# Attention plus mixture of experts on one core: batch 1's scores without stacks, a new order for the first six periods, dummies on TensorE, and a joined router operand

## What is computed

```python
def _L0_xattn_ref(Q, K, V, W_Q, W_K, W_V, W_O):      # 8 heads of 16
    q = proj_split(Q, W_Q); k = proj_split(K, W_K); v = proj_split(V, W_V)
    scores = jnp.einsum('bhqd,bhkd->bhqk', q, k) / jnp.sqrt(jnp.float32(dh))
    attn = jax.nn.softmax(scores, axis=1)             # over the heads
    ctx = jnp.einsum('bhqk,bhkd->bhqd', attn, v)
    ctx = ctx.transpose(0, 2, 1, 3).reshape(b, s, d)
    return jnp.einsum('bsd,ed->bse', ctx, W_O)
...
x = x + _L0_xattn_ref(_layernorm(x), ctx_1024, ctx_1024, W_Q, W_K, W_V, W_O)
# experts: E = 8, the best 2 of each token, hidden width 256
logits = jnp.einsum('btd,de->bte', x, Wr) + br
topv, topi = jax.lax.top_k(logits, K)
gates = jax.nn.softmax(jnp.where(sel_mask, logits, neg_inf), axis=-1)
h = jax.nn.relu(jnp.einsum('btd,edh->bteh', x, W1) + b1)
out = jnp.einsum('bte,bteh,ehd->btd', gates, h, W2) + jnp.einsum('bte,ed->btd', gates, b2)
x = x + out                                           # its input is _layernorm(x)
```

## Time and profile before

| | us |
|---|---|
| median of 3 runs | 211.32 (210.55 to 213.79) |
| the profiled execution, its own time | 210.83 |
| span of the profiled execution, first to last instruction | 209.0 |
| VectorE busy in it | 166.0 |
| ScalarE busy in it | 132.3 |
| GpSimd busy in it | 110.0 |

### The profile page before, as it was taken

The page is one execution under the profiler, slowest core; times in us unless marked ns, Lnnn a source line. Parts: engine busy times, 40 slices in busy tenths (PEclk is TensorE's granted clock), DMA queues, the critical chain, the costliest instruction groups (busy, mean ns, idle before and its releaser), DMA issues.

```text
span 209.0 us, 4976 instructions
## 1 busy us (share of the span) xinstructions
PE 199.0 (95%) x1752; PEld 176.3 (84%) x1752; DVE 166.0 (79%) x445; ACT 132.3 (63%) x316; POOL 110.0 (53%) x132
## 2 busy tenths in 40 slices
PE   6999888698999999999999999999999999999994
PEld 6846775686899889997999799988998999789993
DVE  5398779889789999988888988798989978365542
ACT  2236847796578858687668767575767685345541
POOL 8603657869795475439661966285738672010000
PEclk9999999999999999999999999999999999999999
DMA  6549695725434233424241306050000000000000
GB/s 195 137 137 291 178 266 161 206 86 159 109 102 100 78 100 105 102 75 104 98 106 53 124 14 183 13 175 4 0 3 25 0 2 28 0 3 2 28 0 25
DMA packets 20248, 18.70 MB, mean 89 GB/s; under 512 B 1760, under 2 KB 18688, under 8 KB 20224
## 3 DMA queue, kind: packets, MB, share of 16 engines
q1 hardware_dynamic: 17472, 16.91, 28.2%
q10 hardware_dynamic: 2752, 1.48, 2.7%
HBM read 11.83 MB, written 6.55 MB: 88 GB/s over the span
## 4 chain that ended last, share of the span: by engine, by line
PE 91%; DVE 3%; ACT 2%; issue 1%; POOL 1%; DVEq 0%; POOLq 0%; ACTq 0%
PE y_ps L416 28%; PE h_ps L403 21%; PE score_ps L343 7%; PE misc_ps L362 6%; PE score_ps L331 6%; PE h_ps L351 4%; PE score_ps L265 3%; PE misc_ps L300 2%; PE misc_ps L383 2%; PE score_ps L320 2%; PE score_ps L403 2%; PE misc_ps L371 1%; PE misc_ps L270 1%; PE misc_ps L309 1%; PE misc_ps L289 1%
## 5 line engine op out<-in xcount | busy, mean ns | idle before, releaser
L670 ACT ACTIVATE hT<-h_ps,b_sb 128x256 f32<-128x256 f32 x118 | 49.4, 470 | 34.5 <-PE h_ps L403 33.4
L416 PE MATMUL y_ps<-w_sb,hT 128*128 128x128 f32 x512 | 68.4, 276 | 0.0
L416 PEld LDWEIGHTS y_ps<-w_sb,hT 128*128 128x128 f32 x512 | 63.3, 191 | 3.4 <-issue 2.0
L1152 POOL TENSOR_TENSOR half_sum<-e_sb 128x512 f32<-128x512 f32 x28 | 36.9, 1320 | 34.0 <-ACT e_sb L642 33.6
L911 DVE TENSOR_TENSOR attn<-e_sb,e_rcp 128x1024 f32<-128x1024 f32 x32 | 42.8, 1341 | 3.5 <-ACT e_rcp L653 3.3
L903 DVE TENSOR_REDUCE shift_m<-score_ps 128x128 fp32r<-128x1024 f32 x32 | 38.7, 1213 | 2.4 <-PE score_ps L331 1.2
L403 PE MATMUL h_ps<-x1T_hi,w_lo 128*128 128x256 f32 x118 | 37.7, 320 | 1.3 <-ACT hT L670 0.6
L642 ACT ACTIVATE e_sb<-score_ps 128x1024 f32<-128x1024 f32 x32 | 32.8, 1024 | 5.4 <-PE score_ps L343 5.2
L974 DVE SCALAR_TENSOR_TENSOR acc<-y_ps,gates,acc 128x128 f32<-128x128 f32 x96 | 29.0, 343 | 8.3 <-PE y_ps L416 6.9
L403 PE MATMUL h_ps<-x1T_lo,w_hi 128*128 128x256 f32 x118 | 33.1, 280 | 0.0
L403 PE MATMUL h_ps<-x1T_hi,w_hi 128*128 128x256 f32 x118 | 33.0, 279 | 0.0
(11 more groups left out here) (113 smaller groups left out, 286.8 us busy)
## 6 DMA issues: line engine op xcount, KB each, us to landing
k_scratch<-k_parts SPq DMA_DIRECT2D x14, 256.0 KB, 2.6
k_stack<-k_scratch SPq DMA_DIRECT2D x14, 256.0 KB, 4.0
q_stack<-q_scratch SPq DMA_DIRECT2D x28, 128.0 KB, 2.7
q_scratch<-q_parts SPq DMA_DIRECT2D x7, 256.0 KB, 2.5
w_sb<-in_w SPq DMA_DIRECT2D x1, 1024.0 KB, 6.5
out_y<-y_out SPq DMA_DIRECT2D x8, 128.0 KB, 1.9
x_all<-in_x ACTq DMA_DIRECT2D x1, 768.0 KB, 6.0
ctxT<-in_ctx_t SPq DMA_DIRECT2D x1, 640.0 KB, 5.5
```

Source lines behind the costliest of these rows:

```text
L416: mm = nc.tensor.matmul(y_ps[:, j % 2, t * D:(t + 1) * D], hT[:, j % 2, c, t * P:(t + 1) * P], w2_sb[:, e * HC + c, :], start=(c == 0), st ...
L670: op = nc.scalar.activation(hT[:, j % 2, c, :], hidden(j)[:, c * S:(c + 1) * S], ACT.Relu, bias=b1_sb[:, e * HC + c:e * HC + c + 1])
L1152: nc.gpsimd.tensor_tensor(half_sum[:], e[:, 0:HQ // 2], e[:, HQ // 2:HQ], ALU.add).then_inc(sum_step, 1)
```

## The change

- `FIRST = 2`: batches 0 and 1 both go through `first_scores`, with `k_first` and `q_wide` for two batches. Batch 1 is no longer split, spilled and loaded; all semaphore counts of the stacks move by one.
- The router's high and low weights lie side by side in `wr_pair`. For each token tile, one matmul of high x by both (16 columns) and one of low x by the high half. `take_logits` adds the two parts in two steps.
- SP issues w1 and the rest of ctx once x of batch 1 and ctx of batch 1 have landed, and then spills and loads for batch 2; the load of k follows the spill of q. The clearing of `q_stack[1]` on GpSimd goes from before `v_pad` to after the third norm.
- `ln1` runs batch by batch (before: batches 3, 4 together and 5, 6, 7 together).
- `keep_warm` takes a place and a wait. There are 18 dummies behind the first 12, at seven places, for 8 at three.
- `beginning()` is laid out anew on TensorE, ScalarE, VectorE and GpSimd. `period(i)` keeps its order.

```diff
-    PE_SUMS = 4
+    FIRST = 2
+    PE_SUMS = (0, 1, 2, 3,)
...
@@ sync
-            spill_k(1)
+            sp.wait_ge(x1_in, 16)
+            sp.wait_ge(ctx_in[1], 16)
             sp.dma_start(w1_sb[:], w1.rearrange("e d h -> d e h")).then_inc(w1_in, 16)
-            load_k_stack(1)
-            spill_q(1)
-            load_q_stack(1)
+            sp.dma_start(ctxT[:, 3:B, :], ctx_t[3:B].rearrange("b d s -> d b s")).then_inc(ctx_rest_in, 16)
             spill_k(2)
-            sp.dma_start(ctxT[:, 3:B, :], ctx_t[3:B].rearrange("b d s -> d b s")).then_inc(ctx_rest_in, 16)
+            spill_q(2)
             load_k_stack(2)
-            spill_q(2)
             load_q_stack(2)
...
@@ tensor
                 for t in range(TT):
-                    tok = slice(t * P, (t + 1) * P)
-                    for k, (xt, w) in enumerate(((x1T_hi, wr_lo), (x1T_lo, wr_hi), (x1T_hi, wr_hi))):
-                        mm = nc.tensor.matmul(misc_ps[:, S + t * E:S + (t + 1) * E], xt[:, b % 2, tok], w[:],
-                                              start=(k == 0), stop=(k == 2), skip_group_check=True)
+                    tok, at = slice(t * P, (t + 1) * P), S + 2 * t * E
+                    nc.tensor.matmul(misc_ps[:, at:at + 2 * E], x1T_hi[:, b % 2, tok], wr_pair[:].rearrange("p k e -> p (k e)"),
+                                     start=True, stop=False, skip_group_check=True)
+                    mm = nc.tensor.matmul(misc_ps[:, at:at + E], x1T_lo[:, b % 2, tok], wr_pair[:, 0, :],
+                                          start=False, stop=True, skip_group_check=True)
                 mm.then_inc(logits_done, 1)
...
@@ vector
+                parts = misc_ps[:, S:S + 2 * TT * E].rearrange("p (t k e) -> p t k e", k=2, e=E)
+                nc.vector.tensor_tensor(logits_part[:], parts[:, :, 1, :], br_sb[:].unsqueeze(1).to_broadcast([P, TT, E]),
+                                        ALU.add).then_inc(logits_step, 1)
+                dve.wait_ge(logits_step, b + 1)
+                nc.vector.tensor_tensor(logits[:], parts[:, :, 0, :], logits_part[:], ALU.add).then_inc(logits_made, 1)
```

More of the change, by code:

```diff
@@ L262, in _, with keep_warm @@
         def _(pe):
-            def keep_warm(n):
-                for _ in range(n):
-                    nc.tensor.matmul(score_ps[:, 1, 0:P], ident[:], ident[:], start=True, stop=True, skip_group_check=True)
+            def keep_warm(times, dst, freed, n):
+                wait(pe, freed, n)
+                for _ in range(times):
+                    nc.tensor.matmul(dst, ident[:], ident[:], start=True, stop=True, skip_group_check=True)
             def project_k(b, freed, n):
@@ L535, in beginning @@
[L535 to L539 removed]
+                project_q(3, v_taken, 4)
+                expert_down(0, 1)
                 scores(2, 3)
                 subtract_max(2, 2)
[L542 removed]
+                expert_up(0, 3)
+                attend_values(1, q_lo_made, 2)
+                project_out(1, heads_taken, 2)
@@ L543, in beginning @@
+                expert_down(0, 2)
+                expert_up(0, 4)
+                project_k(4, x1_made, 2)
+                expert_up(0, 5)
+                subtract_max(2, 3)
+                transpose_x1n(1, k_lo_made, 3)
                 expert_down(0, 3)
-                expert_up(0, 5)
-                project_k(4, x1_made, 2)
+                scores(3, 0)
+                transpose_xn(4, x1T_lo_made, 2)
                 expert_down(0, 4)
-                scores(3, 0)
+                gated_b2(0, xnT_taken, 5)
@@ L559, in beginning @@
-                project_v(3, xnT_taken, 5)
+                project_v(4, q_lo_made, 3)
                 expert_down(0, 7)
-                project_q(4, v_taken, 4)
+                subtract_max(3, 1)
+                attend_values(2, v_taken, 5)
                 expert_up(1, 1)
+                route(1, heads_taken, 3)
                 expert_down(1, 0)
-                project_v(4, q_lo_made, 4)
                 expert_up(1, 2)
-                subtract_max(3, 1)
+                project_k(5, logits_made, 2)
```

434 lines of the change are left out of this document (204 added, 230 removed).

## The result

The change makes the kernel slower by one per cent: 213.31 us (median of 4 runs, 212.97 to 214.64) after 211.49 (4 runs, 210.55 to 213.79), ratio 1.010 [1.006, 1.014]. The profiled execution of after has a span of 211.3 us, before 209.0.

The account below looks back on a forecast made before the run. TensorE was taken to set the end almost everywhere, with room only in the ramp. 209.0 - 1.8 (layout) - 1.3 (router) = 205.9 us span, 207.7 as execution, 208.2 us as median; range 204.5 to 212.0.

Parts of the forecast that it names:

- the layout: New order of the ramp on all engines: period 6 opens at 79.65 instead of 81.44, 1.8 us ahead.
- Router: Router matmuls on TensorE, four weight loads instead of six: 0.22 us less per batch, 1.3 us over six loop periods.
- Scores in fp32: Batch 1's four score units in the ramp: 2.0 us more on TensorE, 0.5 on VectorE, no trip through DRAM.
- DMA order: SP's earlier w1 and ctx transfers: the last x load may land later, bounds 0 and 1.1 us, taken as 0.
- The third rival: Batch 2's stacks land late, past 37.0 each us costs a us; slower, 214.8 us if at 43.5; chance 0.08.
- The walk: Ramp stepped through in program order on all engines with the old trace's durations, giving each stage's start.
- the first part: Ramp up to the first expert: it starts at 40.3 against 41.05 for the work done, 0.75 us ahead.
- The second: Ramp from first expert to period 6: 1.05 us gained, with TensorE waits of 0.6, 0.65 and 0.65.
- Dummies at 0.1 us: Nine new dummies in mid-ramp stand before waits: 0.1 us at the first three, nothing at the others.
- They buy nothing: Dummies in the ramp: the clock stayed full through gaps of 1.42 and 1.09 us without them; clock fall given 0.02.
- The ramp gives nothing: Rival: dearer scores and 2.1 us of dummies eat the ramp's gain, only the router is left: 210.0 us; chance 0.17.
- Slower than before: Whole kernel slower than the old one, most of it inside 2%; chance 0.10.

Follow-up runs that it names:

- e1: The kernel before with only the router changed: four matmuls instead of six and two adds for the logits; 210.24 us, 0.991 of before.
- e2: The kernel before, old order, router and dummies, with batch 1's scores in fp32 and SP's new transfer order; 210.62 us, 0.995 of before.
- e4: The changed kernel with the first norm's epsilon added by GpSimd instead of VectorE; 213.28 us, 1.004 of before.
- e5: The kernel before, in its old order and with its old dummies, with batch 1's fp32 scores and the joined router; 209.40 us, 0.985 of before.
- e9: The changed kernel with expert_up(0,4) moved on TensorE between attend_values(1) and project_out(1); 1.007 of before.
- f2: The changed kernel with batch 0's gates as early as in the old order, and expert_down(0,2) and expert_up(0,4) between attend_values(1) and project_out(1); 1.009 of before.
- e3: The changed kernel without its nine dummies in mid-ramp; 1.010 of before.
- e10: The changed kernel with batch 0's way to its x1n put first on all engines, and two dummies less; 1.015 of before.
- e7: The changed kernel with the norm statistics of batches 5 and 6 and the router weights' split moved off VectorE's way to the first expert; 1.009 of before.
- f1: The changed kernel with expert_up(0,0) directly behind batch 0's x1n transposes, its relu early, and the router weights split earlier on VectorE; 1.008 of before.

## Why the prediction was wrong

The forecast of 208.2 us missed by 5.1, and one term, the layout, has an error of 5.4.

- *Router: right.* -0.22 for each of six periods, 1.3 in all. The matmuls start 0.11 apart, and the periods take 22.12 us after 22.34; e1 gains with it alone. The second small add cost nothing.
- *Scores in fp32: cheaper than thought.* Their 2.0 us on TensorE lay in the gaps: e2 opens period 6 0.4 us sooner than before.
- *DMA order: right.* The stacks of batch 2 came at 37.08 for 36.5. TensorE idled 0.50 us for them, but the x1n transposes behind waited for x1n in any case (ScalarE made it until 39.10). The third rival did not occur. x took 6.3 us to land for 6.0, and nothing waited for it.
- *The walk up to 25 us: right* within 0.4 us: 9.68 for 10.1, 17.41 for 17.5, 25.22 for 25.2. q_lo(2) was to be done at 28.1 and was at 28.98, 0.9 late: this is where it starts to fail.
- *The layout, 1.8 ahead: this is the step that failed.* It was 3.6 behind. By its own account, the first part was to be 0.75 ahead (first expert at 40.3 against 41.05) and was 1.3 behind (42.33). The second was to gain 1.05 and lost 2.3. Three things were wrong in it.
  - *Durations.* The walk took them from undisturbed rows. From 25 to 35 VectorE was busy 9.7 of 10 us, and two epsilons of 0.89 and 0.94 us for 0.17 and a normalisation of 1.67 lay on the way: `attend_values(0)` came 0.8 late (31.84 for 31.0), the x1n transposes 1.7 (39.24 for 37.55). e4 shows that taking such stalls away returns only 0.3 us there, 0.6 with its slower start taken off, since TensorE's order is next.
  - *Its arithmetic.* It allows the second part 1.6 us by steady packing and names two waits of 0.65 in it. That leaves a gain of 0.3 and not 1.05.
  - *The waits behind `attend_values(1)`.* The walk has two of 0.65. In after there are three, 0.65, 0.27 and 0.59, and e5, the old order, has none from there to period 6: 32.2 us for 30.8. So this stretch lost 1.4 us where the walk counts on a gain. Moving a pair (e9, f2) moves the waits: 1.83 and 1.32 us of them, at other places.
- *The extra chains of `ln1`* had no price in the walk. In the old order they cost 1.9 to 2.1 us; what they cost in the new one no run tells.
- *Dummies at 0.1 us: right.* By e3, seven of the nine in mid-ramp cost nothing and the other two have a wait behind them. *"They buy nothing": wrong.* One profiled execution had a full clock; half the runs of before had not, and without the nine the clock falls to 0.55.
- *The rivals.* "The ramp gives nothing" (210.0) came nearest, and its sign (period 6 after 81) is there at 85.02, but its reasons, dearer scores and dummies, were both wrong. That the new order might be plainly worse than the old one, with no wait above over 0.74 us, was no case of its own. Slower than before got 0.10.

What stays open: of the 4.4 us between e5 and after, 2.0 are there at the values of batch 0, 3.0 at those of batch 1 and the last 1.4 are the three waits behind them. e10 names 0.86 of the first 2.0. How the rest divides between order, split statistics and stalls was not settled; with VectorE and TensorE both nearly full there, no single move (e4, e7, e9, e10, f1, f2) brought period 6 more than 0.7 us forward.

The version that beats both kernels is e5, the old order with both edits: 209.40 us, 0.985 [0.978, 0.991], and 0.991 at full clock.
